# Windowed attention in blocks of 32 queries instead of 64, with the rotation finished on VectorE and the roots on GpSimd

## The reference

```python
def attn_layer(x, Wqkv, qs, ksc, Wo):          # six layers
    q, k, v = split heads of (x @ Wqkv)
    q = l2norm(q) * qs;  k = l2norm(k) * ksc
    q = q * cos * scale + rotate_half(q) * sin * scale
    k = k * cos / scale + rotate_half(k) * sin / scale
    out = local_attention(q, k, v)             # softmax(8 q.k, masked to key <= query <= key + 32) @ v
    return out @ Wo
def ffn_layer(x, g, bln, W1, b1, W2, b2):
    xn = layernorm(x) * g + bln
    a, gate = split(xn @ W1 + b1)
    return a * gelu(gate) @ W2 + b2
for i in range(6):
    x = attn_layer(shift_tokens(x), ...) + x
    x = ffn_layer(shift_tokens(x), ...) + x
```

## Time and profile before

| | |
|---|---|
| median of 3 runs | 2546.63 us (2536.71 to 2547.93) |
| profiled execution, own time | 2536.73 us |
| its span | 2535.0 us |
| mean granted TensorE clock | 0.965 |
| busy over the span: TensorE, VectorE, ScalarE, GpSimd | 2325.2, 2004.9, 1850.2, 1277.4 us |
| one round of the last stage | 69.7 us |

### The profile page before, as it was taken

How to read it: one execution, slowest core, us unless ns; L and a number is a source line. 1 busy time by engine, 2 the same in 40 slices (tenths; PEclk the granted TensorE clock), 3 DMA queues, 4 the chain that set the end, 5 groups by cost and what they waited for, 6 DMA issues and landing times.

```text
span 2535.0 us, 60549 instructions
## 1 busy us (share of the span) xinstructions
PE 2325.2 (92%) x22196; PEld 1663.6 (66%) x22196; DVE 2004.9 (79%) x4390; ACT 1850.2 (73%) x4176; POOL 1277.4 (50%) x1093
## 2 busy tenths in 40 slices
PE   6798689999966899999999999999999999999996
PEld 3476368888754666666666666666667666666762
DVE  2599477777777888888888898888888888888862
ACT  2255478888744788877888888887788788878772
POOL 0132010000005877776777777776777677766650
PEclk8899799999987999999999999999999999999997
DMA  2000112221002111012111111102111111111110
GB/s 86 9 2 1 44 69 75 75 75 67 27 22 77 35 30 38 25 39 56 41 39 33 52 41 27 39 25 56 41 39 39 50 35 33 27 51 44 25 29 21
DMA packets 37812, 103.90 MB, mean 41 GB/s; under 512 B 7953, under 2 KB 13393, under 8 KB 34705
## 3 DMA queue, kind: packets, MB, share of 16 engines
q1 hardware_dynamic: 37520, 100.04, 13.8%
HBM read 50.61 MB, written 2.23 MB: 21 GB/s over the span
## 4 chain that ended last, share of the span: by engine, by line
PE 40%; DVE 16%; ACT 4%; issue 3%; DMA 3%; POOL 3%; SPq 1%; DVEq 0%; ACTq 0%; POOLq 0%
PE w_psP L1766 12%; PE w_psO L1816 6%; PE w_psF L1713 4%; PE w_psA L1799 4%; PE w_psF L1734 4%; PE w_psT L1773 3%; PE w_psS L1789 3%; DVE w_rs L67 2%; DVE w_bb L1915 2%; DVE w_ab L1914 2%; DVE w_sm L1937 2%; PE w_psF L1738 2%; PE w_psS L1783 1%; DVE w_mx L1931 1%; DVE w_nrm L1921 1%
## 5 line engine op out<-in xcount | busy, mean ns | idle before, releaser
L2006 POOL TENSOR_TENSOR w_ab<-w_ab,w_bb 128x512 f32<-128x512 f32 x384 | 491.9, 1284 | 210.5 <-DVE w_bb L1915 210.4
L2011 POOL TENSOR_TENSOR w_ab<-w_ab,w_nrm 128x512 f32<-128x512 f32 x384 | 397.7, 1052 | 125.1 <-DVE w_nrm L67 125.1
L1866 ACT ACTIVATE w_pb<-w_psS,w_mx 128x96 f32<-128x96 f32 x1536 | 391.2, 360 | 3.3 <-DVE w_mx L1931 2.6
L1842 ACT ACTIVATE w_sq<-w_psP 128x512 f32<-128x512 f32 x384 | 232.0, 604 | 157.5 <-PE w_psP L1766 152.1
L2016 POOL TENSOR_TENSOR w_pb<-w_pb,w_sm 128x768 f32<-128x768 f32 x192 | 282.4, 1471 | 111.6 <-DVE w_sm L1938 111.6
L1766 PE MATMUL w_psP<-w_hi,w_xh 128*128 128x512 f32 x576 | 300.6, 522 | 24.8 <-DVE w_bb L1915 12.2
L1914 DVE TENSOR_TENSOR w_ab<-w_psP,w_tabs 128x512 f32<-128x512 f32 x384 | 263.1, 685 | 63.9 <-ACT w_sq L1842 56.9
L1931 DVE TENSOR_REDUCE w_mx<-w_psS 128x4 f32<-128x384 f32 x384 | 201.7, 547 | 115.5 <-PE w_psS L1789 115.5
L1873 ACT ACTIVATE w_pT<-w_psA 128x512 f32<-128x512 f32 (+1 forms) x384 | 233.0, 607 | 64.0 <-PE w_psA L1799 63.2
L1921 DVE TENSOR_REDUCE w_nrm<-w_sq 128x8 f32<-128x512 f32 x384 | 258.7, 674 | 5.9 <-ACT w_sq L1842 3.8
L1915 DVE TENSOR_TENSOR w_bb<-w_psP,w_tabs 128x512 f32<-128x512 f32 x384 | 261.3, 681 | 0.0
(11 more groups left out here) (300 smaller groups left out, 5094.8 us busy)
## 6 DMA issues: line engine op xcount, KB each, us to landing
e_gb<-gate_rows SPq DMA_DIRECT2D x16, 1024.0 KB, 4.7
X<-tables_layer SPq DMA_DIRECT2D x48, 256.0 KB, 3.5
X<-w_v SPq DMA_DIRECT2D x48, 256.0 KB, 3.1
e_raw<-in_w_moe SPq DMA_DIRECT2D x32, 256.0 KB, 5.2
w_raw<-in_w_qkv SPq DMA_DIRECT2D x20, 384.0 KB, 3.7
X<-tables_layer SPq DMA_DIRECT2D x48, 128.0 KB, 3.1
w_o<-in_w_o SPq DMA_DIRECT2D x6, 512.0 KB, 4.6
w_xs<-H SPq DMA_DIRECT2D x24, 128.0 KB, 2.2
```

Of the source, the lines that this page charges most:

```text
L1866: last = act.activation(pb[k % 2][:, 4 * j + q, WIN * (k % 2):], psS[j][:, q * KEYS:(q + 1) * KEYS], ACT.Exp, bias=mx[:, 4 * j + q:4 * j + ...
L2006: pool.tensor_tensor(a, a, bb[:, i % 2, :], ALU.add).then_inc(s["ad"], 1)
L2011: pool.tensor_tensor(a, a, nrm[k // 2][:, 1, 8 * (i % 8):8 * (i % 8) + 8].unsqueeze(2).to_broadcast([128, 8, DH]), ALU.mult).then_inc(s["n ...
```

## The change

Attention still goes in eight blocks of a round, but a block is now two windows of 32 queries of one tile (an even block takes windows 0 and 2, an odd one 1 and 3), each with 64 keys, for all 16 heads: the 128 rows hold four heads of 32 queries, the columns two banks of four slots of 64 keys. So a score block is 32 products of 32 x 64 in eight 64x32 tiles (eight mask products of 32 x 256 before them); one row maximum over both banks; exponentials of 64 columns that also put out their sum, so that `Xd` is the reciprocal alone; GpSimd scales 128 x 512; one group of four transposes, into `psT`, which both kinds of transposes now share; and a value product of 32 products of 64 x 32 in four 64x64 tiles, which use two banks `psO`. `v_even` has 128 rows.

In `AB`, VectorE multiplies the swapped halves into `bb`, multiplies the projection's bank by the cosine table in place, and adds the two into `ab`; the first two operations are linked. GpSimd's `ad` goes. The inverse roots of the norms (`Ra`) and of the layer norm (`lr`) are done on GpSimd, in twelve linked operations each (`rsqrt_simple`); the layer norm on VectorE is split in `ls` (statistics) and `ln` (scaling). The orders of all five engines are written anew. The x that is read back at the end waits for less.

```diff
+def rsqrt_simple(eng, ch, y, x, half, tmp, first, op):
+    def two(out, in0, a, b, op0, op1):
+        ch.link(eng.tensor_scalar(out, in0, float(a), float(b), op0, op1))
+    def times(out, in0, in1):
+        ch.link(eng.tensor_tensor(out, in0, in1, ALU.mult))
+    two(half, x, first, 0.5, op, ALU.mult)
+    two(y.bitcast(I32), half.bitcast(I32), -0.5, GUESS, ALU.mult, ALU.add)
+    times(tmp, y, y)
...
+    times(y, half, y)
...
-    qpos, kpos = np.tile(np.arange(64), 2)[:, None], np.arange(-32, 64)[None, :]
+    qpos, kpos = np.tile(np.arange(32), 4)[:, None], np.arange(-32, 32)[None, :]
...
-    PAIRS, BLK = HEADS // 2, 64
-    KEYS = WIN + BLK
-    NBLK = N // BLK
+    PAIRS, QB, KEYS = HEADS // 2, 32, 64
+    NBLK = 2 * TILES
...
-    pb = [c.sb(f"w_pb{j}", [128, PAIRS, KEYS + WIN * j]) for j in range(2)]
+    pb = [c.sb(f"w_pb{j}", [128, PAIRS, KEYS]) for j in range(2)]
...
-    pT = c.sb("w_pT", [128, PAIRS, 128])
+    pT = [c.sb(f"w_pT{j}", [128, 4, 128]) for j in range(2)]
...
-    psA = c.ps("w_psA")
-    psS = [c.ps(f"w_psS{j}") for j in range(2)]
-    psO = c.ps("w_psO")
+    psS = c.ps("w_psS", (128, 2, 512))
+    psO = c.ps("w_psO", (128, 2, 512))
...
         "pe": """
+            V2.1- T1.1- P3.0- S1.0- Av7.0-- T1.2- P3.1- P3.2- T1.3- wo0-- P3.3- S2.0- At0.0- V3.0- wo1--
+            V3.1- At1.0- P0.0 S3.0- T2.0- P0.1 T2.1- Av0.0- T2.2- P0.2 tr-- T2.3- Av1.0- T3.0- P0.3
+            S4.0- T3.1- V0.0 At2.0- V0.1 P1.0 At3.0- back-- S5.0- T3.2- P1.1 Av2.0- T3.3- P1.2 g0--
+            S6.0- At4.0- P1.3 a0-- Av3.0- V1.0 S7.0- At5.0- Av4.0- At6.0- g1-- V1.1 P2.0 Av5.0- At7.0-
+            a1-- T0.0 P2.1 T0.1 g2-- T0.2 P2.2 T0.3 Av6.0- S0.0 a2-- P2.3 T1.0 V2.0 w2--""",
...
         "dve": """
+            out--- R2.3- Xd0.0- AB3.0- Xm1.0- R3.0- AB3.1- R3.1- R3.2- AB3.2- Xd1.0- R3.3- Xm2.0- AB3.3-
+            Xd2.0- xf-- R0.0 AB0.0 Xm3.0- R0.1 AB0.1 AB0.2 ls-- AB0.3 Xm4.0- Xd3.0- ln-- R0.2 R0.3
...
         "pool": """
+            nm2.1-- nm2.2-- nm2.3-- Xn2.0-- nm3.0-- nm3.1-- lr--- Xn3.0-- nm3.2-- nm3.3-- Xn4.0-- wl0.0-
+            Xn5.0-- Xn6.0-- Ra0.0- Xn7.0-- nm0.0- nm0.1- nm0.2- nm0.3- nm1.0- nm1.1- xl0.0 nm1.2- nm1.3-
+            Xn0.0- Xn1.0- Ra1.0- nm2.0-""",
...
-                        sp.wait_ge(s["p"], r * UP)
+                        sp.wait_ge(s["p"], (DEPTH - 1) * NB * UP)
...
-                    sp.dma_start(v_even[k % 2][WIN:KEYS, :], v[k][0:BLK, :]).then_inc(s_ve[k % 2], 16)
+                    sp.dma_start(v_even[k % 2][WIN:128, :], v[k][0:128 - WIN, :]).then_inc(s_ve[k % 2], 16)
...
                 elif kind == "T":
-                    wait(pe, s["te"], r * UR + 4 * k + j)
+                    if psT_free:
+                        pe.wait_ge(*psT_free[-1])
+                    psT_free.append((s["te"], r * UR + 4 * k + j + 1))
...
                 elif kind == "S":
+                    for c4 in range(4):
+                        for h in range(2):
+                            rows = slice(64 * h, 64 * h + QB)
+                            pe.matmul(psS[QB * c4:QB * c4 + QB, h, 0:4 * KEYS], c.ident_bf[rows, rows],
+                                      c.band_bf[rows, min(k, 1), :], start=True, stop=False, skip_group_check=True)
...
+                    for g in range(2):
+                        for n in range(2):
+                            at = QB * (e + 2 * n)
+                            slot = KEYS * (2 * g + n)
+                            for c4 in range(4):
+                                for h in range(2):
+                                    rows = slice(64 * h, 64 * h + 64)
+                                    last = pe.matmul(psS[QB * c4:QB * c4 + QB, h, slot:slot + KEYS],
+                                                     qT[t % 2][rows, 4 * g + c4, at:at + QB],
+                                                     kT[rows, 4 * g + c4, 128 * t + at:128 * t + at + KEYS], start=False,
+                                                     stop=True, skip_group_check=True)
...
                 elif kind == "At":
-                    wait(pe, s["pte"], r * UA + 2 * k + j)
+                    if psT_free:
+                        pe.wait_ge(*psT_free[-1])
+                    psT_free.append((s["pte"], r * NBLK + k + 1))
...
                 elif kind == "Av":
+                    for h in range(2):
+                        for c4 in range(4):
+                            for g in range(2):
+                                for n in range(2):
+                                    rows, head = slice(64 * n, 64 * n + 64), 2 * (4 * g + c4) + h
+                                    last = pe.matmul(psO[64 * g:64 * g + 64, n, QB * (4 * h + c4):QB * (4 * h + c4 + 1)],
+                                                     vals[rows, head * DH:(head + 1) * DH],
+                                                     pT[k % 2][rows, 2 * h + g, QB * c4:QB * c4 + QB], start=True, stop=True,
+                                                     skip_group_check=True)
...
                 elif kind == "Xe":
+                        last = act.activation(pb[k % 2][:, n, :], psS[:, j, KEYS * q:KEYS * (q + 1)], ACT.Exp,
+                                              bias=mx[:, n:n + 1], accum_out=sm[k % 2][:, n:n + 1])
...
                 elif kind == "AB":
-                    wait(dve, s["ad"], r * UR + i - 1)
                     dve.wait_ge(s["sq"], r * UR + i + 1)
-                    dve.tensor_tensor(ab[...], src, tab[0], ALU.mult)
-                    dve.tensor_tensor(bb[...], src[:, :, ::-1, :], tab[1], ALU.mult).then_inc(s["ab"], 1)
+                    turned = bb[:, i % 2, :]
+                    ch = Chain(dve, s_rope, 2, r * UR + i)
+                    ch.link(dve.tensor_tensor(turned.rearrange("p (h x d) -> p h x d", x=2, d=32), src[:, :, ::-1, :], tab[1],
+                                              ALU.mult))
+                    ch.link(dve.tensor_tensor(src, src, tab[0], ALU.mult))
+                    ch.end()
+                    dve.tensor_tensor(ab[:, k % 2, j, :], psP[j % 2][:, :], turned, ALU.add).then_inc(s["ab"], 1)
...
                 elif kind == "Xd":
-                    ch.link(dve.tensor_reduce(sm[k % 2][:, :], pb[k % 2][:, :, WIN * (k % 2):], AX_X, ALU.add))
                     dve.reciprocal(sm[k % 2][:, :], sm[k % 2][:, :]).then_inc(s["r"], 1)
...
-                elif kind == "ad":
-                    pool.tensor_tensor(a, a, bb[:, i % 2, :], ALU.add).then_inc(s["ad"], 1)
...
+                elif kind == "Ra":
+                    rsqrt_simple(pool, ch, nn[:, 1, :], nn[:, 0, :], nn[:, 2, :], nn[:, 3, :], 1e-24, ALU.max)
...
+                elif k == "lr":
+                    rsqrt_simple(pool, ch, rs[:, 0, :], mv[:, :, 1], rs[:, 1, :], rs[:, 2, :], 1e-5, ALU.add)
```

More of the change, by code:

```diff
@@ L1555, in windowed_layers @@
     s_ve = [c.sem(f"w_s_ve{j}") for j in range(2)]
-    s_norm, s_sum, s_f = (c.sem("w_s_chain_" + k) for k in ("norm", "sum", "tail"))
+    s_norm, s_stats, s_root, s_rope = (c.sem("w_s_chain_" + k) for k in ("norm", "stats", "root", "rope"))
     def load_scl(sp, layer):
@@ L1742, in _ @@
         def _(pe):
+            psT_free = []
             def free(u, r):
@@ L1776, in step @@
                 elif kind == "S":
[L1777 removed]
+                    t, e = k // 2, k % 2
                     pe.wait_ge(s["te"], r * UR + 4 * t + 4)
[L1779 to L1784 removed]
@@ L1785, in step @@
[L1785 to L1792 removed]
+                    wait(pe, s["e"], r * UE + 2 * k)
```

167 lines of the change are left out of this document (72 added, 95 removed).

## The result

The changed kernel takes **2629.5 us** in the median (2625.3 to 2636.8), the kernel before beside it 2545.3: **3.5% slower**, ratio 1.035 with an interval of 1.032 to 1.037. The forecast was 2409 us and the range ended at 2545. The profiled execution took 2631.9 us with a span of 2630.1, 95.1 more than the span before. I take the differences from these two spans; the medians differ by 84.

What follows compares the result with a forecast made beforehand. TensorE was taken as the bound, VectorE a close second. TensorE's 59.3 us plus 4.7 of stalls gave a round of 64.0 instead of 69.7, 137 less over 24 rounds: 2400 profiled, 2409 in the median; range 2325 to 2545.

Steps and rivals of the forecast that it cites:

- TensorE's work: Scores, transposes and value products on TensorE: 1.1 us less per block, 8.8 per round, from 68.1 to 59.3.
- The value product: On TensorE, 64 records of 32 columns, four at a time: 0.68 us instead of 1.22, 0.54 less per block.
- The score block: On TensorE, mask and scores in eight tiles at a time: about 0.83 us, 0.12 less per block.
- The waits: Stalls allowed in a round on top of the highest loads: 4.7 us, where 1.6 were seen before.
- the shared bank of the transposes: TensorE may refill it only after ScalarE's copy: 0.1 to 0.2 us each time, 2 to 5 us per round.
- the copies of value rows: Transfers on SP's queue, same number, grown from 64 to 96 rows, issued a tile ahead: costed at nothing.
- covered by the second bank while VectorE is below 90%: The projection's bank, held 0.83 us longer by VectorE's rotation, 16 times, was to cost TensorE nothing.
- Exponential and read: On ScalarE, each exponential of 64 columns with its accumulator read: 0.32 us a pair, 64 per round, 5.4 us more.
- The rotation's three operations: On VectorE, two products and their sum: 2.02 us, 0.83 more, 16 times, 13.3 us per round.
- Rival 2: Issue of small products on TensorE is the bound, a floor of 20.6 ns a record: 2662 us; chance 0.10.
- Rival 3: ScalarE becomes the bound, exponential and accumulator read not overlapping, 0.52 us a pair: 2628 us; chance 0.07.
- Rival 1: No gain on TensorE: small products run as now, or shared-bank waits replace them; 2481 to 2560 us; chance 0.18.

Runs made afterwards that it cites:

- e5: The changed kernel with only the first 32 of each head's 64 value columns as weights of the value products; 2608.9 us, ratio 1.027.
- e1: The changed kernel with the output weights of a new layer loaded right behind the last output product of the old one; 2588.3 us, ratio 1.019.
- e10: The changed kernel with a new layer's output weights loaded early and the second half of block 0's exponentials earlier on ScalarE; 2584.4 us, ratio 1.017.
- e12: The kernel before with each mask product of 384 columns written as eight of 48; 2553.3 us, ratio 1.004.
- e14: The kernel before with the scores of block 1 four units earlier in TensorE's order; 2568.9 us, ratio 1.012.

## Why the prediction was wrong

**TensorE's work, the step that failed first.** The prediction took scores and value products by their moving columns alone and divided these by the number of tiles. The value product went wrong most: "I take 0.50 and the tail of 0.18, 0.68 instead of 1.22" measured 1.07. The rows of both units in the changed kernel, at full clock:

```profile
1744.96 0.30 PE L1805 MATMUL w_psS<-band_bf,ident_bf 32*32 32x256 bf16 x8
1745.19 0.86 PE L1814 MATMUL w_psS<-w_kT,w_qT 64*32 64x64 f32 x64
1745.98 0.66 PE L1795 MATMUL w_psT<-tables_all,w_ab 128*128 128x128 f32 x4
...
1747.26 1.14 PE L1843 MATMUL w_psO<-w_pT,X 64*64 64x32 f32 x64
1748.32 0.66 PE L1795 MATMUL w_psT<-tables_all,w_ab 128*128 128x128 f32 x4
```

The pace of the value product is 58 ns for four records, set by 64 weight columns (e5). The earlier trace rows could not show this, since there a value product has 64 columns on either side. The score block was to take 0.83 and takes 1.02 (0.23 from mask to scores, 0.79 to the next unit). The eight tiles do run together at first, 56 ns for the second and third group of eight records, but the second half of the unit takes 12 ns a record in the mean and doesn't keep up; why is not shown. The transposes saved their 0.43. Together 0.07 - 0.16 - 0.43 = -0.51 a block, so 4.1 us a round and not 8.8. This is 4.7 of the 10.0 us by which a round missed (73.98 against 64.0); 0.2 more is that the average round before has 68.3 us of work and not the 68.1 of the earlier trace rows.

**The waits.** TensorE was to stall 4.7 us a round. It is idle 7.3, which is 2.6 more. I had looked for them at the shared bank of the transposes, 2 to 5 us a round; its waits (for w_kT, 12.2 us in the kernel, and smaller ones) are 18 us in 24 rounds, 0.7 a round, so that term was too large. What I had not priced: that the scores of a block need the bank of the block before, whose exponentials stand behind other work in ScalarE's new order (53.9), the output weights, which the new order of units asks for before they are there (27.9, and by e1 41 us in all), GpSimd's scaled probabilities before their transposes (23.3), the copies of value rows that I "cost [...] at nothing" (9.9), and the breaks within units (22.1), which are the supply of instructions.

**The clock.** No part of the prediction had it. The busy time is 66.65 a round, where the work before less 4.1 would be 64.2; I take the 2.4 more for what passes at half clock. It is a remainder and not measured by itself; its size fits, since 116 us of the 19 rounds are at half clock, 6.1 a round, and at most half of that, about 3, is lost (an estimate). 4.7 + 0.2 + 2.6 + 2.4 are the 10.0 within 0.1.

In differences: the 19 rounds take 66.7 us more where 108 less were forecast (19 times 5.7), so they miss by 175; what lies around them takes 28.4 more where 29 less were forecast, 57. Together that is the 232 between the profiled 2631.9 and the forecast of 2400 for it.

**The filling.** Forecast at nothing, it costs 29.0 us. There VectorE is what TensorE waits for, from the first projections on (22.1 us for w_ab against 10.1 for w_bb before), so the third operation of the rotation shows. That is 12 of the 29.0; the half clock is the other part that I can name, 47 us of the filling against 23 before. The cover that I named for the longer hold, "covered by the second bank while VectorE is below 90%", holds in the rounds but for 11.9 us, and not there.

**Right.** Exponential and read were to take 0.32 and take 0.29, by the distance from one pair to the next. The rotation's three operations were to take 2.02 and take 2.03 in the median, writing to PSUM in place costs next to nothing extra (700 ns against 681 and 691), GpSimd's operations came out under the forecast, and the wait for the layer norm, 28.3 us before, is 6.2. The loads of the other engines hold: per round VectorE 54.4 (54.2 forecast), ScalarE 57.7 (58.7), GpSimd 36.8 (39.8). The one that bounds the kernel is the one that does not.

**The rivals.** The outcome, slower by 3.5%, had a chance of 0.19 and none of its mechanisms did it. Rival 2, an issue floor, was to decide from 16 ns a record; records pass at 10 ns in the score unit and 15 in the value unit. But its kind was right in part, as the later half of each score unit and the breaks show. Within a group, records of different tiles start 7 ns apart (3 in the score unit before), so the 25 ns from start to start that the Trainium skill states (TensorE: Matmul & The Clock Gate, "Wait — 56ns, not 53.3ns?") are no floor across tiles. Rival 3 gives 2628, close to the measured time by chance: its pair was to take 0.52. Rival 1 comes nearest, the gain not there and waits in its place, but it was priced to end at 2560.

**What stays open.** Whether an order of units exists in which the change gains. e10 is the best that was found with its parts, 2584. Why the second half of a score unit is slower than the first. And what lowers the clock: whether taking away one wait of each pair would keep it up, and what stands behind the 7 falls of 21 without such a pair.

## What to carry over

Price a group of small matmuls in different tiles by the longer of its two sides, weight columns and moving columns, and ask which of the two a smaller block makes shorter: halving the queries of a block left the value columns, and so the time, as they were. In a kernel whose units stand in an order written by hand, a gain in one engine's work is not a gain in time until each handover of the new order is priced: take the distance between what a unit needs and when it is ready, unit by unit. And a saving from smaller tiles is bought with records, here 55% more of them on TensorE, which has its own price in the supply of instructions: lay the landings of the instruction fetches beside any idle time for which no engine is responsible.

## What the hardware showed that I had not expected

- Four value records in different tiles pass in 58 ns with 64 weight columns and in 33 ns with 32, at the same 32 moving columns and 64 rows.
- Within a group, records of different tiles start 7 ns apart; over a whole score unit the mean is 10 ns, and about 12 in its second half.
- Units can break for 0.2 to 2 us, and such a break ends 1.25 to 1.57 us after the landing of a 16 KB instruction fetch: 21 times in the changed kernel, and likewise 5 times in e12 (1.28 to 1.52) and 30 in e5 (1.2 to 1.65), never in the kernel before.
- A single wait of 1.33 us a round in a full TensorE cost its length alone and no half clock (e14); single ones of 1.24 to 1.98 us stand before 4 of the 21 falls of the changed kernel.
